# Attention scores 2.5 heads ahead, contiguous queries, and row maxima turned through DRAM

## The reference

```python
h = _modulate(_layernorm(x), shift_msa, scale_msa)
qkv = (h @ W_qkv + b_qkv).reshape(b, l, 3, H, D)
scores = jnp.einsum('blhd,bmhd->bhlm', q * scale, k)
attn = jax.nn.softmax(scores, axis=-1)
o = jnp.einsum('bhlm,bmhd->blhd', attn, v).reshape(b, l, c)
```

## Time and profile before

| | us |
|---|---|
| median of 3 runs | 3323.84 |
| the profiled execution | 3319.47 |
| its span, first to last instruction | 3317.8 |
| attention within it (first load of a head to last store) | 718 to 1922 |
| busy in the span: PE, DVE, POOL, ACT | 2939.1, 1698.6, 1525.1, 1400.5 |

### The profile page before, as it was taken

The page is one execution under the profiler, slowest core; times in us unless marked ns, Lnnn a source line. Parts: engine busy times, 40 slices in busy tenths (PEclk is TensorE's granted clock), DMA queues, the critical chain, the costliest instruction groups (busy, mean ns, idle before and its releaser), DMA issues. The chain is left out here.

```text
span 3317.8 us, 49285 instructions
## 1 busy us (share of the span) xinstructions
PE 2939.1 (89%) x16066; PEld 2386.0 (72%) x16066; DVE 1698.6 (51%) x2862; ACT 1400.5 (42%) x1758; POOL 1525.1 (46%) x1143
## 2 busy tenths in 40 slices
PE   6759899968999999999999966849999999999976
PEld 2248777745666666666666645739999999999975
DVE  3446566546887888788887758741111111111125
ACT  2122222216888888888888822211111111111112
POOL 1232222115888878888888848752222222222210
PEclk9769899978999999999999978869999999999988
DMA  5365565552333333333333245658111121121144
GB/s 179 122 234 201 188 217 203 201 150 48 78 68 81 70 76 79 67 80 71 74 80 67 52 161 206 244 201 263 35 54 49 35 69 35 37 67 35 49 141 140
DMA packets 351132, 373.72 MB, mean 113 GB/s; under 512 B 179985, under 2 KB 243097, under 8 KB 350990
## 3 DMA queue, kind: packets, MB, share of 16 engines
q1 hardware_dynamic: 343512, 359.12, 36.4%
q10 hardware_dynamic: 7482, 12.69, 1.3%
HBM read 221.81 MB, written 149.36 MB: 112 GB/s over the span
## 5 line engine op out<-in xcount | busy, mean ns | idle before, releaser
L752 POOL TENSOR_TENSOR a_pl<-a_pf,a_ph 128x1024 fp32r<-128x1024 f32 x384 | 913.4, 2398 | 73.3 <-ACT a_pf L823 73.3
L769 DVE TENSOR_REDUCE a_mx<-a_psum_s 128x1 f32<-128x1024 f32 x512 | 625.9, 1222 | 246.4 <-PE a_psum_s L838 246.4
L821 ACT ACTIVATE a_ph<-a_psum_t 128x1024 fp32r<-128x1024 f32 x512 | 525.8, 1027 | 195.3 <-PE a_psum_t L853 195.0
L1407 POOL TENSOR_TENSOR m_al<-m_af,m_ah 128x256 fp32r<-128x256 f32 x288 | 212.1, 737 | 764.6 <-DVE m_ah L1416 764.6
L1455 PE MATMUL m_psum_h<-m_ht,m_w 128*128 128x256 f32 x4032 | 533.9, 284 | 31.7 <-DMA m_w<-w_s 23.0
L1455 PEld LDWEIGHTS m_psum_h<-m_ht,m_w 128*128 128x128 f32 x4032 | 508.5, 189 | 35.1 <-issue 34.0
L1416 DVE CAST m_ah<-m_af 128x256 fp32r<-128x256 f32 x288 | 84.6, 294 | 836.2 <-ACT m_af L1393 836.2
L1469 PE MATMUL m_psum_y<-m_w,m_ah 128*128 128x288 f32 x2304 | 505.2, 296 | 1.4 <-DVE m_y L1433 1.2
L1393 ACT ACTIVATE m_af<-m_psum_h,m_bias 128x256 f32<-128x256 f32 x288 | 137.0, 476 | 813.7 <-PE m_psum_h L1455 813.7
L838 PE MATMUL a_psum_s<-a_ks,a_qs 108*128 108x512 f32 x1024 | 425.0, 497 | 35.0 <-DVE a_mx L769 19.9
L838 PEld LDWEIGHTS a_psum_s<-a_ks,a_qs 108*128 108x128 f32 x1024 | 286.5, 327 | 197.9 <-DVE a_mx L769 171.3
(11 more groups left out here) (213 smaller groups left out, 3158.1 us busy)
## 6 DMA issues: line engine op xcount, KB each, us to landing
a_qs<-q_s SPq DMA_DIRECT2D x192, 144.0 KB
a_ks<-k_s SPq DMA_DIRECT2D x192, 144.0 KB
w_s<-q_ws SPq DMA_DIRECT2D x64, 324.0 KB, 3.4
h_s<-p_ht SPq DMA_DIRECT2D x40, 512.0 KB, 5.1
m_ht<-h_s SPq DMA_DIRECT2D x16, 1280.0 KB, 8.2
v_s<-q_vo SPq DMA_DIRECT2D x64, 288.0 KB, 2.3
a_vs<-v_s SPq DMA_DIRECT2D x128, 144.0 KB
q_s<-q_qko SPq DMA_DIRECT2D x32, 512.0 KB, 2.7
```

The source lines that it names most:

```text
L752: pool.tensor_tensor(pl[:, s % RING], pf[:, s % RING], raw(ph[:, s % RING]), ALU.subtract).then_inc(lo_pool, 1)
L769: dve.tensor_reduce(mx[:, u % 2, t:t + 1], p_s[:], AX.X, ALU.max).then_inc(s_free, 1)
L821: act.activation(ph[:, s % RING], p_t[:, s % 2], ACT.Exp, scale=SCALE)
L1407: pool.tensor_tensor(al[:, f % RING], af[:, f % RING], raw(ah[:, f % RING]), ALU.subtract).then_inc(lo_ready, 1)
```

## The change

The score tiles now take contiguous queries, `t * P:(t + 1) * P`, so `mx[c, t]` belongs to query 128t+c. They are made `2 * KT + EARLY` tiles ahead, EARLY = 4: at step s of head hd PE makes tile s+4 of head hd+2 for s < 4, and tile s-4 of head hd+3 from s = 4 on; 20 tiles instead of 16 come ahead of the first step. POOL splits the maxima of head hd+2 behind s = 4 of head hd instead of those of hd+1 behind s = 0. The way of the maxima has two parts: `send_max` writes `mh` to a DRAM tensor `maxima` by two DMAs whose destination steps element by element (4 bytes each, 1024 each), and `put_max`, later, reads both rows back with one DMA into `qs`. SP's order for head hd becomes: the loads of head hd+3; `put_max(hd+1)`; `store(hd, 0)`; `send_max(hd+2)`; `store(hd, 1)`.

```diff
+    SPLIT_STEP = 4
+    EARLY = 4
+        max_out = [sem(f"max_out{i}") for i in range(SLOTS)]
-                def put_max(hd, u):
+                def send_max(hd, u):
                     sp.wait_ge(mh_lo, hd + 1)
                     for s in range(2):
-                        sp.dma_start(raw(qs[SROWS + s:SROWS + s + 1, u]).rearrange("o (c t) -> o c t", t=KT),
-                                     raw(mh[:, u % 2, s])).then_inc(max_in[u], 16)
+                        sp.dma_start(maxima[u, s].rearrange("(t c) -> c t", c=P), raw(mh[:, u % 2, s]),
+                                     allow_slow_non_contiguous=True).then_inc(max_out[u], 16)
+                def put_max(u, i):
+                    sp.wait_ge(max_out[u], 32 * (i + 1))
+                    sp.dma_start(raw(qs[SROWS:MROWS, u]), maxima[u]).then_inc(max_in[u], 16)
                 load(0, 0)
                 sp.wait_ge(set_up, 2)
                 for hd in range(1, SLOTS - 1):
                     load(hd, hd)
+                send_max(0, 0)
                 put_max(0, 0)
+                send_max(1, 1)
                 def body(hd, u, i, last):
-                    if not (last and u == SLOTS - 1):
-                        put_max(hd + 1, (u + 1) % SLOTS)
                     if not (last and u > 0):
                         sp.wait_ge(p_free, RING + STEPS * hd)
                         load(hd + SLOTS - 1, (u + SLOTS - 1) % SLOTS)
-                    for lh in range(LH):
-                        store(hd, lh)
+                    if not (last and u == SLOTS - 1):
+                        put_max((u + 1) % SLOTS, i + (u + 1) // SLOTS)
+                    store(hd, 0)
+                    if not (last and u >= SLOTS - 2):
+                        send_max(hd + 2, (u + 2) % SLOTS)
+                    store(hd, 1)
 # POOL, body
-                        if s == 0 and not (last and u == SLOTS - 1):
-                            split_max(hd + 1, (u + 1) % SLOTS, i if u == 0 else i + 1)
+                        if s == SPLIT_STEP and not (last and u >= SLOTS - 2):
+                            split_max(hd + 2, (u + 2) % SLOTS, i + 1)
 # DVE, body
-                        if not (last and u + over >= SLOTS - 2):
-                            max_tile(hd + over + 2, (u + over + 2) % SLOTS, s)
+                        later, t = divmod(KT * (over + 2) + s + EARLY, KT)
+                        if not (last and u + later >= SLOTS):
+                            max_tile(hd + later, (u + later) % SLOTS, t)
 # PE
-                        m = pe.matmul(p_s[:, h * 512:(h + 1) * 512], qs[0:SROWS, u, t:L:KT],
+                        m = pe.matmul(p_s[:, h * 512:(h + 1) * 512], qs[0:SROWS, u, t * P:(t + 1) * P],
-                for hd in range(2):
-                    for t in range(KT):
-                        score_tile(hd, hd, 0, t)
+                for t in range(2 * KT + EARLY):
+                    score_tile(t // KT, t // KT, 0, t % KT)
                         values(hd, u, s)
-                        if not (last and u >= SLOTS - 2):
-                            score_tile(hd + 2, (u + 2) % SLOTS, i + (u + 2) // SLOTS, s)
+                        later, t = divmod(2 * KT + s + EARLY, KT)
+                        if not (last and u + later >= SLOTS):
+                            score_tile(hd + later, (u + later) % SLOTS, i + (u + later) // SLOTS, t)
 # build
+    maxima = scratch("maxima", 4, 2, L)
```

More of the change, by code:

```diff
@@ L611, in _, with stage_attention @@
                           .then_inc(ro_ready, 1)
-def stage_attention(nc, q_s, k_s, v_s, o_t, sums):
+def stage_attention(nc, q_s, k_s, v_s, o_t, sums, maxima):
     KT = L // P
@@ L734, in _, with split_max @@
                 pool.memset(raw(ks[:, 1:SLOTS]), -1.0).then_inc(set_up, 1)
-                def split_max(hd, u, puts):
-                    if puts is not None:
-                        pool.wait_ge(max_in[(u + 2) % SLOTS], START + 32 * puts)
+                def split_max(hd, u, sends):
+                    if sends is not None:
+                        pool.wait_ge(max_out[(u + 2) % SLOTS], 32 * sends)
                     wait_alone(pool, s_free, KT * (hd + 1), passed)
@@ L746, in _ @@
                 split_max(0, 0, None)
+                split_max(1, 1, None)
                 def body(hd, u, i, last):
@@ L786, in finish_lo @@
                     dve.tensor_tensor(ob[0:D, lh], p_o[VLO:VW, lh], ob[0:D, lh], ALU.add).then_inc(o_copied[lh], 1)
-                for hd in range(2):
-                    for t in range(KT):
-                        max_tile(hd, hd, t)
+                for t in range(2 * KT + EARLY):
+                    max_tile(t // KT, t // KT, t % KT)
                 for s in DVE_LO:
@@ L793, in _ @@
                         low(0, s)
-                max_tile(2, 2, 0)
+                max_tile(2, 2, EARLY)
                 def body(hd, u, i, last):
@@ L845, in scores @@
                     if s == 0:
-                        pe.wait_ge(max_in[u], START + 32 * (i + 1))
+                        pe.wait_ge(max_in[u], START + 16 * (i + 1))
                     if s >= 2 and s - 2 in DVE_LO:
@@ L2082, in build @@
                   [(w_proj, wproj_s), (w_fc1, w1_s), (w_fc2, w2_s)], state, u_s, rot_s)
-    stage_attention(nc, q_s, k_s, v_s, o_t, sums)
+    stage_attention(nc, q_s, k_s, v_s, o_t, sums, maxima)
     stage_proj(nc, o_t, sums, rsums, x_rows, wproj_s, ada, mod, x2_s, h2_s)
```

## The result

The changed kernel takes 3653.56 us, the median of 5 runs (3645.96 to 3655.11), beside 3325.37 for the kernel before (5 runs, 3322.69 to 3329.69). The ratio is 1.0986, its 95% interval 1.0973 to 1.0998: 328 us slower, where I forecast 166. The profiled execution has a span of 3653.2 us. The mean granted clock of TensorE is 0.886 in it, and was 0.937.

The account below looks back on a forecast made before the run. The tile-maximum loop through single-buffered `p_s` bounded the old kernel, late loads the new. Late loads +160, start +10.3, end -1, unstalled heads -1.7 gave +168 on 3319.47: 3487, median 4.4 higher, forecast 3490 us, range 3410 to 3540.

Parts of the forecast that it names:

- What bounds the kernel: PE's score tile and DVE's row maximum alternate through single-buffered `p_s`: 2.19 us a step, 17.96 us a head before the change.
- contiguous queries: Score tiles waiting for `p_s` take 0.73 instead of 0.87 us; half a head becomes 8.69 instead of 8.97.
- The loads: Head hd+3's loads come about 3 us late for PE in every head: 20.63 us against 17.96, +160 us over 60 heads.
- L to X: From SP's first load issue (L) to PE's start of tile 0 of head hd+3 (X): 8.3 us.
- `put_max` behind the loads: On SP, the read of maxima issued behind the loads costs 0 to 0.5 us a head, taken as 0.
- From the last maximum to L: From the maximum ahead of `finish_lo(hd, 1)` to SP's next first load issue: 2.87 us.
- Start, end: Four more tiles ahead of the first step +10.3 us, fewer at the end -1, three heads without stall -1.7.
- POOL's wait: POOL's wait for a head's last maximum, 175.2 us in 60 pieces, moves and doesn't go; 0 to 0.2 us a head.
- The clock: Rival: TensorE's clock falls in stalls of 3 us, costing hundreds of us; chance 0.03.
- The scatter: The 2048 4-byte writes a head into DRAM take 1.5 us, hidden by the rest of the head: cost 0.
- slow scatter: Rival: 4-byte writes over 66 ns an engine delay the next loads; at 100 ns +258 us, about 3750; chance 0.15.
- X to L: From PE's start of tile 0 of head hd+3 to SP's next first load issue: 12.33 us.

Follow-up runs that it names:

- whole-pieces run: Changed kernel with both maxima written to DRAM in 32-byte pieces, 128 a DMA, instead of 4-byte ones, query order left wrong: 3614.92 us.
- matmuls in the wait: Changed kernel with 32-byte pieces into DRAM (query order left wrong) and 12 useless matmuls on PE ahead of each head's wait for loads: 3501.13 us.
- turned read: Changed kernel with earlier loads, 32-byte pieces out, query order made by the read back, at four places: 3810.92, 3690.08, 3788.54 and 4325.86 us.

## Why the prediction was right in direction and wrong in size

- *What bounds the kernel, contiguous queries*: right. 8.67 for half a head against 8.69, and 32 us for the whole.
- *The loads*: right, and the cause of most of the loss. PE waits once a head at L850 for the group of the values; L to X is 8.06 us in the mean of the whole-pieces run (8.3 forecast). `put_max` behind the loads cost nothing that the waits show, as taken.
- *From the last maximum to L*: 3.2 for 2.87. The 0.3 us between an SP issue and the first load stands in the earlier trace rows too (1517.05 + 1.12 to 1518.48), and I left it out; with the shorter L to X it leaves 0.1 to 0.3 a head, part of the 11 us between 3490 and 3501.
- *Start, end, POOL's wait*: 8 us for 7.6; POOL waits 189.4 us for the maxima in the changed kernel and waited 175.2, so this wait moved and did not go.
- *The clock*: the step that failed. It had 0.03, on the ground that the earlier trace rows show PE busy 0.95 of 2 us at a grant of 1.00. But that window says nothing of what follows it, and it is work in small pieces, not a wait of 3 us without any. In the changed kernel the grant falls in or right behind each such wait (45 of 45 between 850 and 1900) and 3.1 to 6.5 us of the work after it run at 1.2 GHz. Price: the run with whole pieces less the one with matmuls in the wait, 3614.92 - 3501.13 = 114 us, 1.9 us a head, less than the "hundreds of us" of that rival. It stood in the sum at 0, though my own turn had the wait that brings it. The Trainium skill, "TensorE: Matmul & The Clock Gate", "HAM oscillation — how this bites in real kernels", describes a kernel in which each tile waits for a DMA and so each starts throttled. The trace agrees: 0.50 at or right behind the first tile of each turn. I hadn't weighed it.
- *The scatter*: the rival "slow scatter" (0.15) had the mechanism and nearly the size a piece (90 ns, beyond the 66 from which it was to decide), but not the price: +258 at 100 ns. Put at 0 in the sum, it costs 3653.56 - 3614.92 = 39 us with late loads; 92 once the clock is kept up, 267 once the loads are early. Late loads hid most of it, and the slow clock helped: by my sum the scatter is issued at X + 3.7 and the next loads' packets begin at X + 13.2, 9.5 us later, so that 2.2 of the 11.7 us would stand out. In the changed kernel X to L is 2.3 us longer than in the sum, the loads are issued 10.5 us behind the scatter (9.65 to 11.74) and their packets 0.9 later, and L to X is 8.65 for 8.06. The third of the heads with the shortest distance (10.0) has 9.19, the third with the longest (11.0) 8.25; with whole pieces both have 8.1. With the clock kept up the distance is 9.5, and L to X 9.03. The term failed because I took a packet's recorded time for the time that it holds the queue. The Trainium skill, "DMA: Bandwidth & Descriptors", Specifications, makes writes under 512 bytes read-modify-write. The trace fits that for neighbours 4 bytes apart (11.7 us), though no run shows the mechanism, and not for size alone: 32-byte pieces took 1.9 us, and 4-byte pieces in 64 bytes of their own cost nothing (3303.77 beside 3304.79).

The mean turns between 850 and 1850 show where each part lies:

| | L to X | X to L | turn |
|---|---|---|---|
| forecast | 8.3 | 12.33 | 20.63 |
| whole pieces, matmuls in the wait | 8.0 | 12.7 | 20.74 |
| whole pieces | 8.06 | 14.64 | 22.70 |
| changed kernel | 8.65 | 14.66 | 23.31 |

The clock's 1.9 us a head lie wholly in X to L, the work behind the stall, and the scatter's 0.6 in L to X, the landing of the loads.

The sum with both: 3490 + 11 (turn 20.74 for 20.63, and its start) + 114 (clock) + 39 (scatter) = 3654. It closes because each term is the difference of two neighbouring runs; taken in the other order the scatter would have 92 and the clock 60. The range to 3540 left out the clock, and with it the result; 3501 lay inside.

What stays open: what holds the signal of 4-byte writes that lie side by side, and why the turned read lands so late.

## What to carry to other kernels

When work moves earlier, list the inputs it waits for and compare each one's deadline with its place in the issuing queue; 4 steps earlier on PE without 4 steps earlier on SP was enough for 260 us of loss here, without the scatter. Price a stall of TensorE like this one (3 to 4 us in each turn) with the half clock behind it (1.9 us here), not by its length alone. Time a DMA of small pieces from issue to signal, and by what the next DMA on the queue has to wait, not by its packets' records.

## What the runs showed of the hardware that I had not expected

- 2048 writes of 4 bytes side by side into DRAM hold their signal for 10.7 to 11.7 us, and keep the loads issued behind them from their full rate for 11.9 us, though their packets are recorded as done after 2.2 us. In 64 bytes of their own they cost nothing measurable.
- A DMA of 128 pieces of 4 bytes into one row on chip lands in 2.0 us, but its issue takes 0.60 us.
- A stall of PE of 3 to 4 us is followed by 3.1 to 6.5 us of work at a grant of 0.50: 1.9 us a turn.
- A read of 2048 pieces of 4 bytes that turns the maxima takes 10.6 to 13.8 us to its signal.
- Twelve useless matmuls in each stall (2.90 us) made a kernel 114 us faster.
